# Turning the sums of a graph convolution: the small operand y stationary, 512 adjacency columns moving, in passes of 12, 8 and 5 tiles

## What is computed

```
deg = zeros(N).at[src].add(1.0)
dinv = deg ** (-0.5)
loop = arange(N)
src_sl, dst_sl = concatenate([src, loop]), concatenate([dst, loop])
coef = dinv[src_sl] * dinv[dst_sl]
agg = segment_sum(x[dst_sl] * coef[:, None], src_sl, num_segments=N)
return relu(agg @ W.T + b)
```

## Time and profile before

| | us |
|---|---|
| median of 3 runs (lowest to highest) | 1381.39 (1378.52 to 1383.36) |
| the profiled execution | 1373.82 |
| its span | 1372.0 |
| TensorE busy, share of the span | 1209.2, 88% |
| VectorE busy | 853.3, 62% |
| ScalarE busy | 543.1, 40% |
| first product of the convolution's sums starts at | 909.34 |
| VectorE takes out the last pass from | 1190.36 |
| VectorE begins with the threshold at | 1226.96 |

### The profile page before, as it was taken

How to read it: one execution, slowest core, us unless ns; L and a number is a source line. 1 busy time by engine, 2 the same in 40 slices (tenths; PEclk the granted TensorE clock), 3 DMA queues, 4 the chain that set the end, 5 groups by cost and what they waited for, 6 DMA issues and landing times.

```text
span 1372.0 us, 31488 instructions
## 1 busy us (share of the span) xinstructions
PE 1209.2 (88%) x11982; PEld 1044.7 (76%) x11982; DVE 853.3 (62%) x1887; ACT 543.1 (40%) x1293; POOL 372.8 (27%) x310
## 2 busy tenths in 40 slices
PE   6669999899689999999999999938999999832997
PEld 4667777677579999999999999827888888622764
DVE  7999899668877777777778665576002224355121
ACT  1556533344355555555555565543001112120221
POOL 2012232000024535445445322223510111121441
PEclk9979999899889999999999999969999999855999
DMA  7755555001275654556765655679755555310110
GB/s 220 193 146 151 152 162 163 25 32 47 81 211 151 181 152 103 113 139 170 205 172 154 172 143 149 158 241 273 229 159 152 176 164 161 107 67 16 56 56 20
DMA packets 236986, 192.75 MB, mean 140 GB/s; under 512 B 157379, under 2 KB 191144, under 8 KB 236798
## 3 DMA queue, kind: packets, MB, share of 16 engines
q1 hardware_dynamic: 217508, 148.17, 40.1%
q0 software_dynamic: 14848, 37.22, 8.6%
q10 hardware_dynamic: 4474, 5.30, 1.2%
HBM read 130.68 MB, written 62.84 MB: 141 GB/s over the span
## 4 chain that ended last, share of the span: by engine, by line
PE 74%; DVE 12%; DMA 6%; issue 3%; SPq 2%; ACT 1%; POOL 1%; POOLq 0%; DVEq 0%; ACTq 0%
PE ps L1682 9%; PE ps L1691 9%; PE ps L1654 8%; PE ps L1702 8%; PE ps L1746 7%; PE ps L1747 6%; PE ps L1794 3%; PE ps L1806 3%; PE ps L1586 3%; DMA arena<-in_edge_attr_dram 3%; PE ps L1511 2%; PE ps L1726 2%; PE ps L1568 2%; PE ps L1523 2%; PE ps L1527 1%
## 5 line engine op out<-in xcount | busy, mean ns | idle before, releaser
L890 ACT ACTIVATE arena<-ps 75x512 f16<-75x512 f32 x462 | 247.9, 591 | 160.5 <-PE ps L1654 160.5
L1746 PE MATMUL ps<-arena 126*128 126x256 f16 x1100 | 245.2, 275 | 32.0 <-DMA arena<-y_scr,yidx 30.7
L1747 PE MATMUL ps<-arena 126*128 126x256 f16 x1100 | 245.0, 275 | 0.0
L693 POOL DMA_INDIRECT y_scr<-arena,tok_out x64 | 146.3, 2286 | 284.9 <-DVE arena L1285 272.0
L1654 PE MATMUL ps<-arena 128*75 128x128 bf16 x1848 | 154.8, 221 | 3.8 <-DVE arena L1242 3.3
L1242 DVE TENSOR_TENSOR arena<-iob,BB 128x1024 bf16<-128x1024 bf16 x231 | 157.6, 682 | 0.0
L1654 PEld LDWEIGHTS ps<-arena 128*75 128x75 bf16 x1848 | 134.8, 116 | 19.3 <-ACT arena L890 8.4
L1523 PEld LDWEIGHTS ps<-arena 128*128 128x128 bf16 x976 | 106.0, 120 | 54.1 <-DVE arena L1080 47.5
L1746 PEld LDWEIGHTS ps<-arena 126*128 126x128 f16 x1100 | 108.4, 99 | 48.0 <-issue 32.8
L1523 PE MATMUL ps<-arena 128*128 128x65 bf16 x976 | 117.4, 204 | 30.8 <-DVE arena L1080 30.8
L1682 PE MATMUL ps<-arena 128*128 128x128 f32 x1024 | 131.2, 282 | 0.0
(11 more groups left out here) (304 smaller groups left out, 2102.8 us busy)
## 6 DMA issues: line engine op xcount, KB each, us to landing
a_scr<-arena SPq DMA_DIRECT2D x115, 300.0 KB, 4.2
arena<-in_edge_attr_dram SPq DMA_DIRECT2D x122, 256.0 KB, 2.9
arena<-in_L_ffn_w_dram SPq DMA_DIRECT2D x54, 512.0 KB, 4.5
arena<-a_scr SPq DMA_DIRECT2D x44, 315.0 KB
arena<-a_scr SPq DMA_DIRECT2D x44, 283.5 KB
arena<-a_scr SPq DMA_DIRECT2D x44, 189.0 KB
arena<-y_scr SPq DMA_DIRECT2D x24, 256.0 KB, 5.2
X<-in_x_dram ACTq DMA_DIRECT2D x1, 3072.0 KB
```

Source lines behind the costliest of these rows:

```text
L693: eng.indirect_dma_start(y2_d, bass.IndirectOffsetOnAxis(ap=tok_out[:, m:m + 1], axis=0), yb[:, i % 4, :], None, bounds_check=NT * 256 - 1 ...
L890: eng.activation(ev[0:75, m % NEV, 4 * (h % 4):4 * (h % 4) + 4, :], PS[ABANK[h % 3]][0:75, :].rearrange("p (s b) -> p s b", b=128), ACT.Id ...
L1746: eng.matmul(z, lhs, yv[0:KR, k, 0:256], start=(k == 0 and h == 0), stop=False)
L1747: ins = eng.matmul(z, lhs, yv[0:KR, k, 256:512], start=False, stop=(k == KT - 1 and (h == 1 or i == len(tiles) - 1)))
```

## The change

The operands of the sums change places. A chunk of y (126 rows x 128 features) is stationary and up to four tiles' adjacency columns (512) move, so a sum comes out with features on partitions, which is the form that the layer's product wants. Tiles are grouped in sets of 4, 4, 4 | 4, 4 | 3, 2 (`SETS`), each with two banks, one per half of the features (`SBANK`). The passes have 12, 8 and 5 tiles. At step 36 (`LOOP_AT`) of each pass a product of `XB`'s tile with 1024 times the identity (`identY`) adds y itself. At a pass's end ScalarE copies the first half of the features of each set into `AT`, VectorE the second half, and no transposes are left. The layer's product goes tile by tile into two banks in turn (`OBANK[t] + t % 2`), for a pair at k % 6 == 4. Since dinv of a node is now a factor of a column of the turned sum, it is applied behind the layer, in VectorE's instruction that adds the bias (1339 in the changed file), and 1/YS goes into `cWT`. On VectorE the score and the last addition of a pair now stand behind the next pair's bias, residual and statistics (`conv_sums`, `conv_shift`, `conv_weights`). `AB0` goes from 2 to 3: five loads, of 12 tiles each, are issued ahead instead of six of 10.

```diff
@@ -385,10 +383,12 @@
         ca = Cut(arena)
         yv = ca([KT, 512], F16)
         yhl = ca([NT, 512], F16)
-        ab = Cut(arena, HB - NAB * 640)([NAB, 1280], F16)
-        assert HB - NAB * 640 + AB0 * 640 >= ohb_end
+        ab = Cut(arena, HB - NAB * ABW // 2)([NAB, ABW], F16)
+        assert HB - NAB * ABW // 2 + AB0 * ABW // 2 >= ohb_end
         gr = Cut(arena, ca.at)([RG * 2, 512])
-        CT2 = ca([2, 2, 256])
+        assert ca.at + RG * 2 * 512 <= HB - NAB * ABW // 2
+        AT = ca([3, 2, 512])
+        identY = ca([128])
         cz = ca([2, D])
         jk = ca([D])
         wsum = ca([NT])
...
@@ -875,7 +875,7 @@
                     e.wait_ge(p_cols, 4 * h + q + 1)
                     eng.activation(to[:, 512 * q:512 * q + n], PS[4 + q % 2][:, 0:n], ACT.Identity).then_inc(a_cols, 1)
             e.wait_ge(p_once, P_CW)
-            eng.activation(cWT[:, :, :], PS[7][:, :].rearrange("p (a b) -> p a b", b=256), ACT.Identity).then_inc(a_once, 1)
+            eng.activation(cWT[:, :, :], PS[7][:, :].rearrange("p (a b) -> p a b", b=256), ACT.Identity, scale=1.0 / YS).then_inc(a_once, 1)
             def tokens_turned(i):
                 e.wait_ge(p_xT, i + 1)
                 e.wait_ge(p_h2, i - 1)
...
@@ -917,22 +917,23 @@
                     e.wait_ge(p_h2, NS)
                     eng.activation(yhl[:, t, 0:256], XB[:, t, :], ACT.Identity, scale=YS).then_inc(a_yh, 1)
-            for q, pr in enumerate(ALL_PAIRS):
-                a, b, n = pr[0], pr[-1] + 1, 128 * len(pr)
-                for t in pr:
-                    e.wait_ge(v_ev, t + 1)
-                    eng.activation(XB[:, t, :], XB[:, t, :], ACT.Identity, scale=dinv[:, t:t + 1]).then_inc(a_scl, 1)
-                e.wait_ge(p_t3, q + 1)
-                if q > 1:
-                    e.wait_ge(p_conv, ALL_PAIRS[q - 2][-1] + 1)
-                eng.activation(CT2[:, q % 2, :, 0:n], PS[TBANK[q]][:, :].rearrange("p (c n) -> p c n", c=2)[:, :, 0:n],
-                               ACT.Identity).then_inc(a_ct2, 1)
-                e.wait_ge(v_ag3, b)
-                eng.activation(rs[:, a:b], mv[:, a:b, 1], ACT.Sqrt, bias=epsc[:, 0:1]).then_inc(a_rs, 1)
-                e.wait_ge(v_nm3, q + 1)
-                e.wait_ge(a_ct2, q + 1)
-                for t in pr:
-                    normalize(t, a_xh3)
+            q = 0
+            for n in range(len(PASSES)):
+                e.wait_ge(p_k, KT * (n + 1))
+                for g in SETS[n]:
+                    u = SET_OF[g[0]]
+                    if u > 2:
+                        e.wait_ge(p_conv, ALL_SETS[u - 3][-1] + 1)
+                    eng.activation(AT[:, SROOM[u], 0, 0:128 * len(g)], PS[SBANK[u][0]][:, 0:128 * len(g)],
+                                   ACT.Identity).then_inc(a_set, 1)
+                for pr in PAIRS[n]:
+                    a, b = pr[0], pr[-1] + 1
+                    e.wait_ge(v_ag3, b)
+                    eng.activation(rs[:, a:b], mv[:, a:b, 1], ACT.Sqrt, bias=epsc[:, 0:1]).then_inc(a_rs, 1)
+                    e.wait_ge(v_nm3, q + 1)
+                    for t in pr:
+                        normalize(t, a_xh3)
+                    q += 1
             def selected_turned(gi):
                 n = 128 * len(GROUPS3[gi])
...
@@ -1325,19 +1326,28 @@
                     e.hold()
                     e.done(eng.scalar_tensor_tensor(nm[:, a:b], mv[:, a:b, 0], -1.0, rs[:, a:b], ALU.mult, ALU.mult), v_nm2)
-            def conv_pair(q):
+            e.wait_ge(v_c2, 2 * NT)
+            e.hold()
+            e.done(eng.tensor_scalar(identY, ident[:, :], YS, None, ALU.mult), v_once)
+
+            def conv_sums(q):
                 pr = ALL_PAIRS[q]
                 e.wait_ge(ld_w1, 16 * 5)
-                e.wait_ge(p_conv, pr[-1] + 1)
                 for i, t in enumerate(pr):
-                    e.hold()
-                    own(eng.tensor_tensor(cz[:, i, :], PS[OBANK[q]][:, 256 * i:256 * i + 256], cbr[:, :], ALU.add))
+                    e.wait_ge(p_conv, t + 1)
+                    e.hold()
+                    own(eng.scalar_tensor_tensor(cz[:, i, :], PS[OBANK[t] + t % 2][:, 0:256], dinv[:, t:t + 1], cbr[:, :],
+                                                 ALU.mult, ALU.add))
                     e.hold()
                     e.done(eng.scalar_tensor_tensor(X[:, t, :], cz[:, i, :], 0.0, X[:, t, :], ALU.max, ALU.add), v_x3)
                     stats(t, v_ag3)
+
+            def conv_shift(q):
                 e.wait_ge(a_rs, RS3 + q + 1)
-                shift(pr[0], pr[-1] + 1, v_nm3)
-                for t in pr:
+                shift(ALL_PAIRS[q][0], ALL_PAIRS[q][-1] + 1, v_nm3)
+
+            def conv_weights(q):
+                for t in ALL_PAIRS[q]:
                     e.wait_ge(a_xh3, t + 1)
                     e.hold()
                     own(eng.tensor_tensor_reduce(out=jk, in0=XB[:, t, :], in1=wrr[:, :], scale=1.0, scalar=0.0,
...
@@ -1346,20 +1356,19 @@
             q = 0
             for n in range(len(PASSES)):
-                if n:
-                    for _ in PAIRS[n - 1]:
-                        conv_pair(q)
-                        q += 1
                 e.wait_ge(p_k, KT * (n + 1))
-                e.hold()
-                for i, t in enumerate(PASSES[n]):
-                    b, h = accumulator(n, i)
-                    e.wait_ge(v_yl, t + 1)
-                    e.done(eng.scalar_tensor_tensor(XB[:, t, :], PS[b][:, 256 * h:256 * h + 256], 1.0 / YS, XB[:, t, :],
-                                                    ALU.mult, ALU.add), v_ev)
-            for _ in PAIRS[-1]:
-                conv_pair(q)
-                q += 1
+                for g in SETS[n]:
+                    u = SET_OF[g[0]]
+                    if u > 2:
+                        e.wait_ge(p_conv, ALL_SETS[u - 3][-1] + 1)
+                    e.done(eng.tensor_copy(AT[:, SROOM[u], 1, 0:128 * len(g)], PS[SBANK[u][1]][:, 0:128 * len(g)]), v_set)
+                for i in range(len(PAIRS[n])):
+                    conv_sums(q)
+                    if i:
+                        conv_weights(q - 1)
+                    conv_shift(q)
+                    q += 1
+                conv_weights(q - 1)
             e.hold()
...
@@ -1705,25 +1714,15 @@
                 if i < NS:
                     adjacency(before_slot(i, 3), before_slot(i, 4))
-            def conv_turn(q):
-                pr = ALL_PAIRS[q]
-                e.wait_ge(a_scl, pr[-1] + 1)
-                e.wait_ge(v_ev, PASSES[0 if q < 5 else 1 if q < 10 else 2][-1] + 1)
-                e.wait_ge(a_ct2, q)
-                for c in range(2):
-                    for j, t in enumerate(pr):
-                        ins = eng.transpose(PS[TBANK[q]][:, c * 256 + j * 128:c * 256 + (j + 1) * 128],
-                                            XB[:, t, c * 128:(c + 1) * 128], ident[:, :])
-                ins.then_inc(p_t3, 1)
-
             def conv_mm(q):
-                pr = ALL_PAIRS[q]
-                e.wait_ge(a_ct2, q + 1)
-                if q:
-                    e.wait_ge(v_x3, ALL_PAIRS[q - 1][-1] + 1)
-                for j, t in enumerate(pr):
+                for t in ALL_PAIRS[q]:
+                    u = SET_OF[t]
+                    o = t - ALL_SETS[u][0]
+                    e.wait_ge(a_set, u + 1)
+                    e.wait_ge(v_set, u + 1)
+                    e.wait_ge(v_x3, t - 1)
                     for c in range(2):
-                        ins = eng.matmul(PS[OBANK[q]][:, 256 * j:256 * j + 256], CT2[:, q % 2, c, j * 128:(j + 1) * 128],
+                        ins = eng.matmul(PS[OBANK[t] + t % 2][:, 0:256], AT[:, SROOM[u], c, o * 128:(o + 1) * 128],
                                          cWT[:, c, :], start=(c == 0), stop=(c == 1))
                     ins.then_inc(p_conv, 1)
...
@@ -1734,31 +1733,40 @@
                     o = n * KT + k
                     e.wait_ge(ld_ab[o % NAB], 16 * (o // NAB + 1))
                     e.wait_ge(ld_yv[k % NYV], 16 * (k // NYV + 1))
-                    for i, t in enumerate(tiles):
-                        b, h = accumulator(n, i)
-                        if n == 1 and i > 3:
-                            e.wait_ge(v_ev, 6)
-                        if n == 2:
-                            e.wait_ge(v_x3, 10)
-                            e.wait_ge(v_ev, 10 if i < 4 else 12)
-                        z = PS[b][:, 256 * h:256 * h + 256]
-                        lhs = ab[0:KR, (o + AB0) % NAB, i * 128:(i + 1) * 128]
-                        eng.matmul(z, lhs, yv[0:KR, k, 0:256], start=(k == 0 and h == 0), stop=False)
-                        ins = eng.matmul(z, lhs, yv[0:KR, k, 256:512], start=False,
-                                         stop=(k == KT - 1 and (h == 1 or i == len(tiles) - 1)))
+                    for g in SETS[n]:
+                        u, w = SET_OF[g[0]], 128 * len(g)
+                        if u == 4:
+                            e.wait_ge(a_set, 3)
+                            e.wait_ge(v_set, 3)
```

(32 more changed lines are left out.)

42 lines of the change are left out of this document (21 added, 21 removed).

## The result

The changed kernel takes 1358.27 us (median of 4 runs, 1357.21 to 1360.01), the kernel before on the same chip 1380.32 (1378.52 to 1383.36): a ratio of 0.9834, 95% interval 0.9815 to 0.9853, or 22 us less. The forecast was 1358.9 in a range of 1351 to 1371. On another chip, later, the ratio was 0.9849 (0.9815 to 0.9883).

What follows compares the result with a forecast made beforehand. TensorE was taken to bound the sums, waits for data the lead-in, and a chain of engines the end. Terms of -3.9 us up to the last step and -18.6 behind it gave -22.5, from 1381.4 to 1358.9 us, range 1351 to 1371.

Steps and rivals of the forecast that it cites:

- Products: TensorE's sums: same columns in fewer instructions, 512 columns taking 212.3 to 218.2 ns, worth -2.8 us.
- Identity products: TensorE, within the passes: 50 added fp32 128x128 products at 0.23 us each, all on the path, +11.5 us.
- Transposes: TensorE: the transposes of the first 19 tiles disappear, -4.2 us.
- no wait of a pair in the second and third pass: Pass 3: waits of a pair's transposes for ScalarE's scaling disappear, -2.2 us.
- Handover: Pass changes: TensorE's 3.1 us of waits shrink to one of 1.2 to 1.3 us, -1.8 us.
- The lead-in: Steps 0 to 21: slower steps absorb waits for y's data, 10.0 us lost instead of 15.3, -5.3 us.
- rival A: Lead-in: DMA is saturated and longer loads raise the loss to 19.1 us; total 1368.0 us, chance 0.15.
- Rival B: Lead-in: the chain store, gather, step is the ceiling, not DMA; 5.9 us lost, total 1354.8 us, chance 0.10.
- Behind the last step: After the last sums: pairs no longer wait for each other except on VectorE, 18 us instead of 36.6, -18.6 us.
- Rival C: Chain behind the last step stays at 30 us and A holds too; 1380.0 us, no change, chance 0.04.
- D: TensorE's sums: the 98 ns weight load is no longer hidden, +98 us, 1480 us, chance 0.04.
- The signs that I had named: Trace marks of the forecast, among them step 22 near 976 us and the last step done near 1186 us.

Runs made afterwards that it cites:

- e7: Changed kernel with y itself added from its two fp16 parts (100 fp16 products) instead of 50 fp32 identity products: 1356.39 us, ratio 0.9797 to the kernel before.
- e2: Changed kernel without the 50 identity products, so the node's own row is left out of the sum: 1348.45 us, ratio 0.9778 to the kernel before.
- e5: Changed kernel with the lead-in's adjacency loads two steps later in SP's order: 1358.15 us, ratio 0.9790 to the kernel before.
- e8: Changed kernel with the lead-in's adjacency loads four steps later in SP's order: 1353.46 us, ratio 0.9793 to the kernel before.
- e4: Changed kernel with VectorE's old order in a pair, its scores before the next pair's work: 1362.25 us, ratio 0.9881 to the kernel before.
- e3: Changed kernel's turned form with the old passes of 10, 9 and 6 tiles and six loads ahead: 1370.34 us, ratio 0.9933 to the kernel before.
- e9: Kernel before, in its old form, with passes of 12, 8 and 5 tiles and five loads ahead: 1377.36 us, ratio 0.9960 to the kernel before.
- e11: Changed kernel with loads four steps later, y added as fp16, and first-pass tile k's part behind step k: 1345.54 us, ratio 0.9745 to the kernel before.
- e1: Kernel before, unchanged, run again for a second profile: 1378.83 us.

## Why the forecast held, point by point

- **Products** (-2.8): 215.8 ns for 512 columns, between the bounds of 212.3 and 218.2. Steps of 2.59, 1.73 and 1.09 us make 237.8 us for 44 of each, -2.2. Right. The Trainium skill, page "TensorE: Matmul & The Clock Gate", section "Wait — 56ns, not 53.3ns?", had 215.7 for it and 55.8 for 128 columns; the trace agrees with both, and the 57.5 ns of the earlier trace rows was no pace of fp16 products at a stretch (e7).
- **Identity products** (+11.5): 11.16 us, all on the path, as e2 shows. Right. **Transposes** gone (-4.2), and no wait of a pair in the second and third pass (-2.2). Right.
- **Handover** (-1.8): one wait of 1.2 us, forecast at 1.2 to 1.3, none at the second. The wait was right, the gain was not. The 3.1 us of the earlier trace rows count the waits of weight loads and of products at line 1746 together, 1.8 and 1.3; TensorE's products had waited 1.3 us, at the first pass change only. So the term is -0.1.
- **The lead-in** (-5.3): wrong, and this is the step that failed. I had said that a slower step absorbs the wait for y's chain, with 10.0 us lost after 15.3. 15.9 were lost: +0.6 against the profile that I had, and -1.8 against the mean of the three before (17.6). Both parts of "10.0" were too small. The first four steps took 17.3 us instead of 14.75, which lost 6.9 and not 4.4. The twelve behind them, "3.06 us against 2.58", took 969.84 - 929.81 = 40.0 us, 3.34 each, which lost 9.0 and not 5.6 (by its own numbers 5.8). The queues moved 267 GB/s where I had put 286, itself the highest of three profiles of the kernel before (275 to 286); 3.06 x 286 / 267 is 3.28. And 6.2 of the 15.9 us were lost by work below full clock, 3.9 of them behind step 4, where I had named 1.5. TensorE waited less than before, 9.7 us behind the first product against 10.8, and lost that again by the clock. It lies between the forecast and rival A, which put the loss at 19.1, nearer to A, though A's total of 1368.0 did not come out. Why the rate fell stays open, and so does the share of bytes and of the ring in what e5 and e8 gained.
- **Rival B** does not come out: its five steps between release and use are there, and the loss stayed. That the chain store, gather, step bounds nothing is not shown by this, since SP still waited 36.0 us for steps. It leaned on a limit of about 358 GB/s for HBM and one core, which the Trainium skill, page "DMA: Bandwidth & Descriptors", section "Specifications", states. No run here had a mean above 288 over the lead-in, so none shows whether that limit can be reached with these transfers. For rival A I had counted 37 full slices; the row has 34 at nine tenths, and the changed kernel's has 38.
- **Behind the last step** (-18.6): -18.8 by the means, -19.7 against the profile that I had. Right, and for the reason given: 17.1 us from the first copy against 18 forecast, VectorE the bound. One part was wrong: the first products still ran at full clock (1.97 us for the eight instructions of two tiles; only the last tile's took 1.90 for four), so VectorE began 1.8 us behind the last step instead of 2.6. For that case the prediction had given 17. e4 and e3 share it out: 2 us are the order on VectorE, about 3 the tile less. Rival C falls. So does D: 98 ns of weight load stayed hidden.
- **The sum** was luck in part. For an execution like the one that I had profiled, the forecast was 1351.3 us; the changed kernel's took 1360.0, 8.7 more. 5.9 of these are the lead-in, 3.2 a later start of the first product, with nothing foreseen for it, and 1.7 the handover; the products add 0.6. The stretch behind the last step gives 1.1 back and the identity products 0.3, and the 1.3 that are still over have no row. Nearly as much, 9.3 us, lies between profiles and medians: the profile before was 7.6 us under its median, and I had added these 7.6; the profile after was 1.7 above its own. So the terms were 8.7 us too hopeful for the profiled execution, and the 7.6 us added for the median, which the changed kernel's own profile does not need, put the total right again. The signs that I had named say the same: step 22 came at 985 us and not near 976, and the last step was done at 1196 and not near 1186. Against the means of the profiles the change is worth -19.0 us, and 2 to 3 us between these and the medians stay open, within their scatter.

## What to carry to other kernels

Turning a product so that its result is already in the form the next product wants is worth what the chain behind the last product costs, not what the fewer instructions promise: 968 product instructions less gained 2 us, and the three circles of scaling, transpose and copy that went, with a tile less, some 17. Where DMA queues are full ahead of a stage, ask what stands in front of the transfers that are waited for, as bytes in the queues and as waits in the issuing engine's program: moving prefetches four steps back gained 6.6 us in the sums. One profile of a kernel that scatters by 5.6 us in its lead-in, and by 6 in when the lead-in begins, is no base for a term of 5 us; take two. And a sum of waits at a line can count one pause twice, for the weight load and for its product.

## What had not been expected of the hardware

With every queue busy, the rate was not one number. In the 46 us from 3 us behind the first product DMA moved 286, 278 and 275 GB/s in the three profiles of the kernel before; in 52 us of the six kernels with loads of 378 KB in the old order (the change twice, e2, e4, e7, e9) it moved 267 to 277, and where their traces give the landings, stores of y landed after 7.5 to 8.7 us; before, after 5.2 to 6.2. The size alone does not do it: with the same long loads two or four steps later (e5, e8, e11) it was 280 to 288, and in e3, with 315 KB, 271, at 0.92 of the engines' time. A late landing alone does not make TensorE wait either: in e11 stores of y landed after 9.6 us, and gathers cost 1.5. This is e8 from 915 to 967 us (columns as in the earlier trace rows), against 267 for the changed kernel in the same stretch:

```profile
915.00:967.00 52.00, 46.38 (x209) 19.58 (x208) 32.28 (x113) 19.93 (x45) 18.28 (x19) 1.00 0.99 286
```

What in the mix of transfers sets the rate was not tried.

The other thing is the clock behind the last step. It fell at different times in executions of one kernel. In the profile of the prediction the first pair's layer products took 3.78 us at half clock; in e1, behind the same pauses of 2.26 and 0.69 us, they took 1.99 at full clock:

```profile
1200.49 1.99 PE L1726 MATMUL ps<-cWT,arena 128*128 128x256 f32 x8 [0.69 <-ACT arena L928]
```

The stretch behind was 1.8 us shorter there, 35.3 against 37.1: these products are on the old chain. In the turned form the last tile's product ran at half clock in some profiles (1.90 us for four instructions, granted clock 0.56) and at full clock in others, as in e5:

```profile
1203.07 1.13 PE L1725 MATMUL ps<-cWT,arena 128*128 128x256 f32 x4 [1.26 <-DVE X L1342]
```

The stretch behind took 17.4 us in both, since VectorE, and not TensorE, is the bound.
